# Two level products over four array tiles, weight low halves on the vector engine, and a new order at the seam between attention and feed-forward

## The reference, cut to what matters

```python
def step(S, inp):
    qt, kt, vt, gt = inp
    S = S * jnp.exp(gt)[..., None] + kt[..., None] * vt[..., None, :]
    o = jnp.einsum('bhk,bhkv->bhv', qt * scale, S)
    return (S, o)
...
x = x + ga * attn(layernorm(x) * (1 + ca) + sa, wq, wk, wv, wo, wg1, wg2, norm_w)
h = layernorm(x) * (1 + cb) + sb
xr = mu_r * h + (1 - mu_r) * h_prev      # h_prev: the token before
xk = mu_k * h + (1 - mu_k) * h_prev
r = sigmoid(xr @ W_r.T)
k = square(relu(xk @ W_k.T))
x = x + gb * (r * (k @ W_v.T))
```

## Time and profile before

| | |
|---|---|
| median of three runs | 1934.22 us (1932.03 to 1934.77) |
| the profiled execution's own time | 1934.33 us |
| its span (first to last instruction) | 1932.4 us |
| PE busy | 1872.8 us, 97% of the span |
| DVE busy | 1431.2 us, 74% |
| ACT busy | 685.6 us, 35% |
| POOL busy | 485.2 us, 25% |
| one attention block | 40.00 us (start of level 64's product in block 29 to that in block 30: 1260.78 to 1300.78) |

### The profile page before, as it was taken

One profiled execution on the slowest core, in us unless ns is written; L12 is line 12 of the kernel. 1 busy time (PEld: TensorE's weight loads), 2 busy tenths in 40 slices (PEclk: granted clock), 3 DMA queues, 4 the chain that ended last, 5 costly groups with the idle time before them and its releaser, 6 DMA issues.

```text
span 1932.4 us, 52891 instructions
## 1 busy us (share of the span) xinstructions
PE 1872.8 (97%) x23145; PEld 1662.7 (86%) x23145; DVE 1431.2 (74%) x2839; ACT 685.6 (35%) x1268; POOL 485.2 (25%) x346
## 2 busy tenths in 40 slices
PE   5799999999999999999999999996999999999999
PEld 1688999889998999889998999986788888888887
DVE  3477677776777667766777677778798988898886
ACT  2233333333333333333333333333343443444443
POOL 2101121111211121111211121115244444444443
PEclk9899999999999999999999999998999999999999
DMA  7100001000110001000110001001121111111110
GB/s 250 66 2 24 24 24 45 24 24 24 35 35 24 24 24 46 24 24 24 36 34 24 24 23 46 24 24 45 55 74 52 62 66 66 52 59 66 64 57 34
DMA packets 42636, 84.66 MB, mean 44 GB/s; under 512 B 2324, under 2 KB 2856, under 8 KB 42408
## 3 DMA queue, kind: packets, MB, share of 16 engines
q1 hardware_dynamic: 38552, 74.46, 11.2%
q10 hardware_dynamic: 3856, 6.82, 1.0%
HBM read 47.72 MB, written 33.55 MB: 42 GB/s over the span
## 4 chain that ended last, share of the span: by engine, by line
PE 93%; DVE 2%; POOL 1%; issue 1%; ACT 0%; POOLq 0%; DVEq 0%; ACTq 0%
PE bank L1117 62%; PE lvl L1117 9%; PE lvl L1188 4%; PE bank L1213 3%; PE bank L1212 3%; PE bank L1125 3%; PE bank L1220 3%; PE lvl L1198 2%; PE bank L1154 2%; PE bank L1204 1%; PE lvl L1170 1%; PE lvl L1194 1%; POOL hT_lo L503 0%; ACT hF L587 0%; DVE Q L867 0%
## 5 line engine op out<-in xcount | busy, mean ns | idle before, releaser
L130 POOL TENSOR_TENSOR ln_rs<-ln_ve,mhalf 128x2 f32<-128x2 f32 x64 | 72.6, 1135 | 1002.1 <-DVE ln_ve L125 1002.1
L854 DVE TENSOR_TENSOR Tot<-Tot 128x256 f32<-128x256 f32 (+2 forms) x192 | 50.1, 261 | 155.9 <-PE lvl L1188 103.8
L1117 PE MATMUL bank<-hT_hi,wq_hi 128*128 128x256 f32 x512 | 152.6, 298 | 9.5 <-POOL hT_lo L503 9.5
L1117 PE MATMUL bank<-hT_hi,wk_hi 128*128 128x256 f32 x512 | 151.0, 295 | 0.3 <-issue 0.3
L136 DVE TENSOR_SCALAR xn<-xs,ln_mv,ln_rs 128x512 f32<-128x512 f32 x128 | 123.2, 1003 | 32.5 <-POOL ln_rs L130 32.5
L1117 PE MATMUL bank<-hT_lo,wq_hi 128*128 128x256 f32 x512 | 146.4, 286 | 0.0
L1117 PE MATMUL bank<-hT_hi,wq_lo 128*128 128x256 f32 x512 | 146.2, 286 | 0.0
L1117 PE MATMUL bank<-xk_hi,fk_hi 128*128 128x256 f32 x512 | 145.1, 283 | 0.0
L1117 PE MATMUL bank<-xk_lo,fk_hi 128*128 128x256 f32 x512 | 144.9, 283 | 0.0
L1117 PE MATMUL bank<-xk_hi,fk_lo 128*128 128x256 f32 x512 | 144.9, 283 | 0.0
L1117 PE MATMUL bank<-hT_lo,wk_hi 128*128 128x256 f32 x512 | 144.6, 282 | 0.0
(11 more groups left out here) (179 smaller groups left out, 5709.0 us busy)
## 6 DMA issues: line engine op xcount, KB each, us to landing
xs<-in_L_attn_x SPq DMA_DIRECT2D x32, 512.0 KB, 3.8
x_scratch<-xs SPq DMA_DIRECT2D x32, 512.0 KB, 3.1
xs<-x_scratch SPq DMA_DIRECT2D x32, 512.0 KB, 3.6
out<-xs SPq DMA_DIRECT2D x31, 512.0 KB, 2.8
mod_raw<-in_L_wmod SPq DMA_DIRECT2D x6, 1024.0 KB, 16.6
raw_q<-in_L_attn_wq ACTq DMA_DIRECT2D x1, 1024.0 KB, 9.5
raw_k<-in_L_attn_wk ACTq DMA_DIRECT2D x1, 1024.0 KB, 14.5
raw_o<-in_L_attn_wo ACTq DMA_DIRECT2D x1, 1024.0 KB, 19.3
```

Source lines behind the costliest of these rows:

```text
L130: pool.tensor_tensor(out=ln["rs"][:, :], in0=ln["ve"][:, :], in1=mhalf[:, :], op=ALU.pow).then_inc(ln["rstd"], 1)
L1117: last = pe.matmul(dst, lhs(a, s), rhs(b, s), start=(t == 0), stop=(t == len(terms) - 1))
```

## The change

Three edits are made together.

First, the products of levels 32 and 64. At level 32 there were 16 matmuls of 32 result columns that wrote to two of the four array tiles; now the same 16 go to four, odd groups one tile further. At level 64 there were 16 matmuls of 64 columns over two tiles; now there are 32 of 32 columns over four. The results lie elsewhere in PSUM, so ACT copies them in four instructions instead of two (level 32) and two instead of one (level 64).

Second, the feed-forward weights' low halves are made by DVE in pieces of 128x512, four for each weight: those of `fk` and `fr` inside block 30, those of `fv` in the crossing. The low halves of block 0's `xk` and `xr` go from POOL to DVE too. ACT casts `fk` and `fr` earlier. The raw W_v is loaded to where the raw W_k lay, as soon as the four pieces of `fk` are done.

Third, the lists of the crossing are reordered: on PE `fr_rows(1)` comes directly behind level 64's product, and the first state product waits for both r sigmoids; on DVE the shift for k stands behind level 2, the statistics of block 33 behind level 32, and `apply_next` behind the last three pieces of `fv`; on ACT `high(0, "k")` comes ahead of the cast of W_v, and the second r sigmoid ahead of `keys_turned`.

```diff
@@ SP
                     if n == LAST - 1:
-                        sp.wait_ge(mm["gate"], 2 * NB)
+                        sp.wait_ge(fw_lo["k"], KT)
                         sp.dma_start(raw["v"][:, :, :], env["W_v"].rearrange("(k p) n -> p k n", p=P)).then_inc(raw_in["v"], 16)
@@ POOL crossing
                     rstd_o(LAST - 1)
-                    low(0, "k")
-                    low(0, "r")
-                    weight_low("v")
                     add(LAST - 1, 0)
+                    add(LAST - 1, 1)
                     ln_rstd(pool, ln, mhalf, NB + 1)
-                    add(LAST - 1, 1)
@@ POOL
                 for n in range(LAST):
                     attention_body(n)
-                weight_low("k")
-                weight_low("r")
                 crossing()
@@ ACT attention_body
                     v_copy(n + 1, 1 - par, 0)
+                    if n == LAST - 1:
+                        weight_high("k")
                     spread_diagonal(n)
...
                     g1_high(n + 1)
+                    if n == LAST - 1:
+                        weight_high("r")
                     for ch in range(chunks_kept(n)):
                         keys_turned(n, ch)
-                    if n == LAST - 1:
-                        weight_high("k")
@@ ACT crossing
+                    high(0, "k")
                     weight_high("v")
-                    high(0, "k")
                     high(0, "r")
...
-                    keys_turned(n, 0)
                     ka_high(0, 0)
                     ka_high(0, 1)
+                    r_sigmoid(0, 1)
+                    keys_turned(n, 0)
                     h2_affine(1, TT)
                     high(1, "k")
-                    r_sigmoid(0, 1)
@@ DVE
+                def weight_low(name, quarters):
+                    hi, lo = F[name]
+                    dve.wait_ge(fw_hi[name], 1)
+                    for k in quarters:
+                        dve.tensor_tensor(out=lo[:, k, :], in0=raw[name][:, k, :], in1=hi[:, k, :].bitcast(F32),
+                                          op=ALU.subtract).then_inc(fw_lo[name], 1)
@@ DVE attention_body
+                        if n == LAST - 1 and m in (8, 32):
+                            weight_low("k", [m // 32])
                     apply_next(n + 2)
                     g1_low(n + 1)
+                    if n == LAST - 1:
+                        weight_low("k", [2, 3])
                     if n > 0:
                         wo_scale(n - 1, 0, bank[3])
+                    if n == LAST - 1:
+                        weight_low("r", [0])
                     gated(n, 0)
@@ DVE crossing
-                    shift(0, "k")
                     level_update(n, par, 2, 2)
                     level_merge(n, par, 2, 2)
+                    shift(0, "k")
                     level_update(n, par, 4, 3)
                     level_merge(n, par, 4, 3)
-                    shift(0, "r")
+                    low(0, "k")
                     level_update(n, par, 8, 4)
                     level_merge(n, par, 8, 4)
+                    shift(0, "r")
...
+                    low(0, "r")
+                    weight_low("v", [0])
+                    level_update(n, par, 32, 6)
                     wo_scale(n - 1, 1, bank[1])
-                    level_update(n, par, 32, 6)
                     ln_stats(dve, ln, n + 2)
+                    level_update(n, par, 64, 7)
                     ln_var(dve, ln, n + 2)
-                    level_update(n, par, 64, 7)
-                    apply_next(n + 2)
                     square(0, 0)
                     square(0, 1)
+                    weight_low("v", [1, 2, 3])
+                    apply_next(n + 2)
@@ PE level_product
-                                quad = slice(32 * b, 32 * b + 32)
-                                last = pe.matmul(dst[quad, g * 32:(g + 1) * 32], k[:, g, quad], q[:, g, b + 1, :], start=True, stop=True)
+                                tile = slice(32 * (b + g % 2), 32 * (b + g % 2) + 32)
+                                last = pe.matmul(dst[tile, g // 2 * 32:g // 2 * 32 + 32], k[:, g, 32 * b:32 * b + 32], q[:, g, b + 1, :],
+                                                 start=True, stop=True)
                         else:
...
+                            for c in range(2):
+                                for b in range(2):
+                                    tile = slice(32 * (b + 2 * c), 32 * (b + 2 * c) + 32)
+                                    last = pe.matmul(dst[tile, g * 32:g * 32 + 32], k[:, g, 32 * b:32 * b + 32], q[:, g, 2 + c, :],
+                                                     start=True, stop=True)
@@ PE crossing
                     level_product(n, par, 7)
+                    pe.wait_ge(y_sb, 2 * n - 1)
+                    fr_rows(1)
...
-                    pe.wait_ge(y_sb, 2 * n - 1)
+                    pe.wait_ge(r_sig, 2)
                     state_step(n, par, 0)
...
-                    fr_rows(1)
```

More of the change, by code:

```diff
@@ L509, in add @@
                     pool.tensor_tensor(out=dst, in0=dst, in1=y[:, ch, :], op=ALU.add).then_inc(x2_sb, 1)
-                def weight_low(name):
-                    pool.wait_ge(fw_hi[name], 1)
-                    pool.tensor_tensor(out=F[name][1][:, :, :], in0=raw[name][:, :, :], in1=F[name][0][:, :, :].bitcast(F32),
-                                       op=ALU.subtract).then_inc(fw_lo[name], 1)
-                def low(m, name):
-                    part, full, hi_s, lo_s = (xk, xk32, xk_hi, xk_lo) if name == "k" else (xr, xr32, xr_hi, xr_lo)
-                    pool.wait_ge(hi_s, m + 1)
-                    pool.tensor_tensor(out=part[1][:, :, :], in0=full[:, :, :], in1=part[0][:, :, :].bitcast(F32),
-                                       op=ALU.subtract).then_inc(lo_s, 1)
                 def gate_b(m, ch):
@@ L637, in merge_32 @@
                     act.wait_ge(mm["lvl"], NL * n + 6)
-                    src = level_bank(6, par)[:, 0:G * 32].rearrange("p (g t) -> p g t", g=G)
+                    src = level_bank(6, par)[:, 0:G * 16].rearrange("p (g t) -> p g t", t=32)
                     for q in range(2):
-                        last = act.copy(A[64 * q:64 * q + 32, :, 64 * q + 32:64 * q + 64], src[64 * q:64 * q + 32, :, :])
+                        for o in range(2):
+                            tile = slice(64 * q + 32 * o, 64 * q + 32 * o + 32)
+                            last = act.copy(A[64 * q:64 * q + 32, o::2, 64 * q + 32:64 * q + 64], src[tile, :, :])
                     last.then_inc(merged_act, 1)
@@ L648, in merge_64 @@
                     act.wait_ge(mm["lvl"], NL * n + 7)
-                    act.copy(A[0:64, :, 64:128], level_bank(7, par).rearrange("p (g t) -> p g t", g=G)[0:64, :, :]).then_inc(merged_act, 1)
+                    src = level_bank(7, par)[:, 0:G * 32].rearrange("p (g t) -> p g t", t=32)
+                    for c in range(2):
+                        last = act.copy(A[0:64, :, 64 + 32 * c:96 + 32 * c], src[64 * c:64 * c + 64, :, :])
+                    last.then_inc(merged_act, 1)
                 def keys_turned(n, ch):
@@ L1192, in level_product @@
                             for b in (0, 2):
[L1193 to L1199 removed]
+                                tile = slice(32 * (b + g % 2), 32 * (b + g % 2) + 32)
+                                last = pe.matmul(dst[tile, g // 2 * 32:g // 2 * 32 + 32], k[:, g, 32 * b:32 * b + 32], q[:, g, b + 1, :],
+                                                 start=True, stop=True)
+                        else:
+                            for c in range(2):
+                                for b in range(2):
+                                    tile = slice(32 * (b + 2 * c), 32 * (b + 2 * c) + 32)
+                                    last = pe.matmul(dst[tile, g * 32:g * 32 + 32], k[:, g, 32 * b:32 * b + 32], q[:, g, 2 + c, :],
+                                                     start=True, stop=True)
                     last.then_inc(mm["lvl"], 1)
```

19 lines of the change are left out of this document (9 added, 10 removed).

## The result

The changed kernel takes 1911.78 us (median of 4 runs, 1910.88 to 1912.48) beside 1933.45 us for the kernel before in the same series (4 runs, 1932.03 to 1934.77). The ratio is 0.9888, 95% interval 0.9876 to 0.9900: faster by 21.7 us. The time is 0.8 us from the forecast of 1911 and inside its range. The profiled execution took 1912.25 us with a span of 1910.5.

The account below looks back on a forecast made before the run. PE's work was taken to bound the blocks, and DVE with POOL on top the crossing. Levels -16.7, block 30 +7.1 and crossing -13.8 sum to -23.4, from the profiled 1934.33 to 1911 us, range 1903 to 1918.

Parts of the forecast that it names:

- Levels, -16.7 foretold: Level products in 31 regular blocks: level 64 saves 0.33 us, level 32 0.22, in all -16.7 us, bounds 11.5 and 17.7.
- The rival of four tiles without a gain: Level products: 32-column instructions stay at 16.1 ns, level 64 takes 1.21 us, total 1931.3, no change; chance 0.07.
- that of a price kept when the width is halved: Level 64: each instruction keeps 28.1 ns, product 1.99 us, +27.9 us, total 1955.5, slower; chance 0.04.
- Block 30, +7.1 foretold: Block 30: fk's late cast makes PE lose 4.6 us, half clock behind it 2.5; bounds 4.6 and 9.
- a stretch in which twelve matmuls lost 2.3 us: Earlier crossing: twelve 512-column matmuls at half clock took 5.25 us instead of 2.94; taken as +2.5 for block 30.
- The crossing, -13.8 foretold: Crossing, counted on DVE: 55.5 us instead of 69.3, -13.8 us, bounds 8 and 19.
- the three small POOL stops: Crossing: POOL's first addition and two gate products each stop DVE for 1.29 us, 3.9 in all.
- the count of DVE's waits: Crossing: two DVE waits left, 1.2 and 1.1 us, instead of 9.3 us of waits before.
- PE's new wait ahead of the state product: Crossing: keys_turned is late behind ka_high and fv's last pieces, so PE waits some 4 us.
- the two that I counted: Crossing, DVE: waits of 1.2 us for the affine of block 1's h2 and 1.1 for the cast of xk.
- the early ones: Crossing: two early gaps of 2.2 and 0.7 us, which might leave PE at half clock.
- the seven long DVE instructions of the earlier trace: Crossing before the change: seven DVE instructions hold 15.4 us more than usual, counted as saved without the large POOL subtractions.

Follow-up runs that it names:

- levels_only: Kernel before with only the new products of levels 32 and 64 and their copies on ACT: 1916.67 us, ratio 0.9911.
- level64_two_tiles: Kernel before with level 64's 64 columns cut into two instructions of 32 on the same two tiles: 1936.74 us, ratio 1.0016.
- fk_cast_early: Changed kernel with ACT's cast of fk moved ahead of block 31's K, f and V copies: 1904.32 us, ratio 0.9848.
- rsig_first: Changed kernel with the second r sigmoid and turned keys ahead of ka_high in ACT's crossing list: 1912.39 us, ratio 0.9890.
- fk_early_tail: fk_cast_early with the second low half of ogT and first wo_scale further up in DVE's list: 1903.56 us, ratio 0.9853.
- fr1_late: Changed kernel with fr_rows(1) back behind fv_rows(0) on PE, and ACT's second sigmoid and turned keys back in place: 1913.06 us, ratio 0.9898.
- the two tails: fk_early_tail (1903.56 us), and the same with the second r sigmoid and turned keys ahead of ka_high (1903.59 us, ratio 0.9849).
- fk_early_rsig_first: fk_cast_early with the second r sigmoid and turned keys also ahead of ka_high on ACT: 1905.53 us, ratio 0.9857.

## Why the prediction came out

The mechanism of each term was the one foretold. That the sum is within 0.8 us is in part luck. The change itself was forecast as -23.4 us and measured as -21.7; 0.9 of the 1.7 between them fell away because the forecast started from the profiled 1934.33 and the series' median is 1933.45. The terms missed by 0.8, 1.0 and 1.8 us in the two traces and in part cancelled; the sizes below are from their cuts.

**Levels, -16.7 foretold.** (0.33 and 0.22 a block make 0.55, not 0.54, so the term should have read -17.1.) -15.1 up to block 30 and -0.84 in it (39.17 without the stall for 40.01) make -15.9; alone, with the crossing's -1.0, they gave -17.3 in levels_only. The products came out at 0.76 and 0.46 us for 0.76 and 0.48. From the start of each product to the start of what follows, 0.57 us is saved in the trace; the block is only 0.50 us shorter. Where the other 0.07 goes isn't located. The rival of four tiles without a gain is excluded by the 0.76 row, and that of a price kept when the width is halved by level64_two_tiles.

**Block 30, +7.1 foretold, +6.1 measured in this trace.** The DVE wait is 6.39 us for 6.4, the PE wait 4.51 for 4.6. What differs is the half clock behind it: I carried over a stretch in which twelve matmuls lost 2.3 us, and here it ended after seven of the twelve, at a loss of 1.5. The term wasn't mis-sized for that. Three other traces with the same wait have the half clock over all but the end of the twelve, and their block 30 is 6.9 to 7.0 us longer than a regular one, which is the forecast. Which of the two a median run has isn't known. fk_cast_early removes exactly this wait and its half clock, and is 7.5 us faster by the medians.

**The crossing, -13.8 foretold, -12.0 measured.** I had DVE at 53.2 us busy and 2.3 us waiting; it was 51.2 busy and 6.2 waiting. The two errors, 2.0 and 3.9 us, go against each other; that only 1.8 is left is luck. There was less work than I had counted: I had put the three small POOL stops at 3.9 us, and they made 2.2, 1.1 on K and 1.1 on the pieces of fv. The one on `ka_low` didn't take place (1.27 us for two, as usual): `ka_low` began at 1341.05 and the gate product that it was to meet at 1341.54, and it was that product which was longer, 1.92 us for 1.29. The step that failed is the count of DVE's waits. I had followed PE's new wait ahead of the state product, but not put it on DVE, which then stands 1.84 us for that product's result:

```profile
1344.17 1.12 DVE L903 SCALAR_TENSOR_TENSOR S<-S,Tot,bank 128x128 f32<-128x128 f32 x4 [1.84 <-PE bank L1234]
```

Two more waits for ACT, 1.16 for h and 1.11 for xk, are the two that I counted. Three short ones that I had at nothing, two for level products and one for `ln_rs`, make 1.65 us, and gaps too short to be listed the last 0.5. The new PE wait itself is 3.1 us for "some 4", and the early ones 2.2 and 0.9 for 2.2 and 0.7. One reading was too wide: of the seven long DVE instructions of the earlier trace rows five stand beside a large POOL subtraction, but K at 1349.05 and the last Tot stand beside an addition and a gate product.

**What the prediction didn't ask** is whether the new wait was worth anything. rsig_first says that it is worth less than 1 us at the crossing's end: with it gone, POOL holds the pieces of fv longer, PE waits for `xn` instead, and the last product falls into half clock.

## What to carry to other kernels

Cost an instruction by what its tile does: with a stationary operand of 32 columns, spreading the same columns over four array tiles instead of two shortened the two products by about a third, while cutting the instructions narrower on the same tiles made it longer. When work is moved into an in-order list, find what it waits for and where that stands in its own list: one cast that stood too late took back 7.5 us of a change worth 29, and moving it up cost nothing. After removing a wait on one engine, look at what its earlier end releases on another: here a sigmoid set a POOL product loose beside the DVE pieces. And before a difference of 1 or 2 us is put down to an edit, compare the stretches that the edit doesn't touch: here one of them differed by 0.9 us.

## What the hardware showed that I had not expected

**Half clock behind equal waits.** fk_cast_early and fk_early_tail have the same wait ahead of the state product. First fk_cast_early, then fk_early_tail:

```profile
1334.20 1.13 PE L1234 MATMUL bank<-V,Kt 128*128 128x128 f32 x8 [3.11 <-ACT Kt L642]
```

```profile
1338.04 2.04 PE L1234 MATMUL bank<-V,Kt 128*128 128x128 f32 x8 [3.13 <-ACT Kt L642]
```

In the first the eight matmuls go at full clock and half clock comes behind them, in the second they are at half clock at once. From the near product to the second output product the second is some 2.6 us longer, 1.3 of it already ahead of the state product, in a stretch that the edit doesn't touch. That profiled execution took 1906.53 us, 3.0 over its kernel's median, so these 2.6 us may be a matter of the execution and not of the kernel. The twelve matmuls in block 30, above, are the clearer case: the same wait, and 0.9 us between the traces. The runs of rsig_first lie 6.9 us apart, and the longest is the one with the lower mean clock. That the clock's timing is behind such spreads in general is argued, not shown; it means that reorderings worth 1 or 2 us in the crossing can't be settled by a few runs or one trace.

**Block times that differ without a change.** With the same instructions in the block, it lasts 39.17 us in the changed kernel, levels_only, rsig_first, fr1_late and the two tails, and 39.11 in fk_cast_early, fk_early_rsig_first and both kernels with fv's low half on POOL: 0.06 us, 1.8 us over 30 blocks. The cause is open.

**Pace of small matmuls.** Over four tiles, 32 columns go at (0.76 - 0.20)/63 = 8.9 ns an instruction, the same as 16 columns there: between 16 and 32 columns on four tiles it is not the columns that set the pace.
